# Indirect transfers of a routed expert layer without a bound: empty slots point at 256 spare rows

## The chip, the cores and the metric

The kernel runs on one core of one Trainium2 chip. The time is device time of one launch in microseconds (us). A core has five engines with instruction streams of their own: TensorE (PE, with its weight loads PEld), VectorE (DVE), ScalarE (ACT), GpSimd (POOL) and SyncE (SP), and 16 DMA engines that move what the queues give them. "POOLq", "SPq" or "DVEq" in a row is the stream of an engine where it does no work of its own kind: it sets a register or issues a transfer.

## The reference

Four blocks follow one another on 4096 tokens (16 x 256) of width 256: causal attention, a ternary feed-forward layer, attention with relative positions, and a layer with 64 routed experts. Only the last one is touched here. Its core, cut to what matters:

```python
scores = jax.nn.sigmoid(x @ gate_w.T)                 # 4096 x 64
topw, topi = jax.lax.top_k(scores, K)                 # K = 8 experts for each token
topw = topw / topw.sum(-1, keepdims=True)
# pos: running number of a token within its expert, C = 256 places for each expert
buf = jnp.zeros((E, C, h)).at[e_flat, pos].set(xin, mode='drop')
g = jax.nn.silu(jnp.einsum('ech,eih->eci', buf, expert_wg))
u = jnp.einsum('ech,eih->eci', buf, expert_wu)
out_buf = jnp.einsum('eci,ehi->ech', g * u, expert_wd)
rows = out_buf[e_flat, pos]
routed = (rows.reshape(T, K, h) * topw[..., None]).sum(1)
return (shared + routed).reshape(b, s, h)
```

There are 64 x 256 = 16384 slots. A token that comes after the 256th of its expert reads the last slot's result. With the inputs of this case the reference's routing puts a token into 11711 slots and leaves 4673 empty: 35 experts are full, 29 are not (one has no token at all).

## The kernel before

`expert_ffn` has two blocks, with a barrier of all engines between them.

The first block (names that begin with m_) works through the tokens in R = 8 rounds of 512. It normalises them, computes gate and shared expert, and writes two tables in device memory: `rows_w`, one row of 320 numbers for each token (256 of the normalised token, 64 gate weights), and `base`, the token plus the shared expert's result. It also makes the map from slots to tokens: `k_token`, 128 x 128 whole numbers, one for each slot. The map comes out of a matmul (`ps_map`), goes through device memory (`slot_map`) to be turned, and three DVE instructions then end the block: an empty slot stands as 0 in the turned map, a filled one as token + 1. `empty` is BIG = 2^20 where the map is below 0.5 and else 0, `map_T` is the sum of both, and `k_token` is `map_T` minus 1. So an empty slot points at row 2^20 - 1. POOL fills the seven buffers `k_rows` with zeros at the end of its part (L1781).

The second block (names that begin with e_) runs over the experts. For expert e the engines do this:

- POOL gathers the rows of its 256 slots with two indirect transfers of 128 rows (L2092, `gather(e)`) into one of seven buffers `k_rows`, 1280 bytes a row. It runs AHEAD = 6 experts ahead.
- PE turns the rows (L2173), multiplies with the expert's three weight matrices (L2184, L2196), which SP loads (L2071 to L2073); ACT and DVE make silu and product between (L2150, L2128).
- ACT copies the result to `e_y`, of which there are two buffers, scaled with the gate weight that stands in the gathered row (L2157). It first waits until the scatter of expert e - 2 has landed.
- POOL adds the result's 256 rows of 1024 bytes into a table of sums with two indirect transfers that accumulate (L2106). Even experts add into `base_scratch`, odd ones into `slots_in_scratch`, so that two experts in flight never add to the same row.

The order on POOL is written out by hand: 6 gathers of two transfers, then for each e the gather of e + 6 and the scatter of e. Each indirect transfer carries a bound:

```python
pool.indirect_dma_start(out=rows[u][:, c, :], out_offset=None, in_=rows_w,
                        in_offset=bass.IndirectOffsetOnAxis(ap=token[:, e * C + c:e * C + c + 1], axis=0),
                        bounds_check=T - 1, oob_is_err=False).then_inc(gathered[u], 16)
```

A row whose number is above the bound is skipped, without an error. The bound is a register, which POOL's stream sets ahead of each transfer (the rows POOLq MOVE of L2092 and L2106).

After the last scatter has landed, both tables are read back, added, completed by the rows of late tokens, and written out (L2080, L2081, L2135, L2140, L2161).

Of the kernel before, what the change touches and what calls it, by code (L numbers as in the profile page):

```python
# [6 lines left out]
F32 = mybir.dt.float32  # L7
# [3 lines left out]
ALU = mybir.AluOpType  # L11
# [3 lines left out]
P = 128  # L15
B, S, D = 16, 256, 256
# [3 lines left out]
T = B * S  # L20
EPS = 1e-5
START = 5
# [29 lines left out]
def bcast(ap, n):  # L52

    return ap.unsqueeze(1).to_broadcast([ap.shape[0], n, ap.shape[1]])
# [1581 lines left out]
def expert_ffn(nc, x3, g_ffn, gate_w, s_wg, s_wu, s_wd, e_wg, e_wu, e_wd, out, slots_in, slots_out, base, pick, weight):  # L1636
# [6 lines left out]
    E, TOP, CAP = gate_w.shape[1], 8, 256  # L1643
    I = s_wg.shape[1]
    G = 4
    R = T // (G * P)
    N = G * P
    C = CAP // P
    K16 = 16
    W = D + E  # L1650
    ROUND = 1.5 * 2.0 ** 23
    BIG = 2.0 ** 20
    rows_w = nc.dram_tensor("rows_w_scratch", (T, W), F32, kind="Internal").ap()
    slot_map = nc.dram_tensor("slot_map_scratch", (E * C, P), F32, kind="Internal").ap()
    sums = [base.rearrange("b s d -> (b s) d"), slots_in[0:T]]
    keep = ExitStack()
    ident = keep.enter_context(nc.sbuf_tensor("k_ident", [P, P], F32))
    late_T = keep.enter_context(nc.sbuf_tensor("k_late_T", [E, T], F32))
    token = keep.enter_context(nc.sbuf_tensor("k_token", [P, E * C], U32))
    ROWS = 7  # L1660
    rows = [keep.enter_context(nc.sbuf_tensor(f"k_rows{i}", [P, C, W], F32)) for i in range(ROWS)]
    with ExitStack() as stack:
# [4 lines left out]
        def sem(name):  # L1667
            sems.append(stack.enter_context(nc.semaphore("m_" + name)))
            return sems[-1]
# [3 lines left out]
        digit = sb("digit", [P, K16], F32)  # L1673
        QE = E // 4
        is_high, is_low = sb("is_high", [P, QE, K16, 4], BF16), sb("is_low", [P, QE, K16, 4], BF16)
        own_p = sb("own_p", [P, 1], F32)
        gate_t = sb("gate_t", [P, ND, E], F32)
        swg, swu, swd = sb("swg", [P, ND, I], F32), sb("swu", [P, ND, I], F32), sb("swd", [I, D], F32)
        gate, tanh_g = sb("gate", [P, 2], F32), sb("tanh_g", [P, 2], F32)
# [29 lines left out]
        weight_ready, late_ready, late_turned, late_copied = (sem("weight_ready"), sem("late_ready"), sem("late_turned"),  # L1709
                                                              sem("late_copied"))  # L1710
        high_ready, low_ready, mapped = sem("high_ready"), sem("low_ready"), sem("mapped")
        blanked = sem("blanked")
        own_ready, tile_ready = sem("own_ready"), sem("tile_ready")
        row_written, base_written = [sem(f"row_written{i}") for i in range(2)], sem("base_written")
        map_ready, map_written, map_loaded, map_turned, token_ready = (
            sem(n) for n in ("map_ready", "map_written", "map_loaded", "map_turned", "token_ready"))
        block = stack.enter_context(nc.Block())
        tiles = lambda a: a.rearrange("b (t p) d -> (b t) p d", p=P).rearrange("(r g) p d -> r p g d", g=G)
        x_rows, base_rows = tiles(x3), tiles(base)
        w_rows = rows_w.rearrange("(r g p) w -> r p g w", g=G, p=P)  # L1720
        wide = lambda a: a[:].rearrange("p g e -> p (g e)")

        @block.sync
        def _(sp):
            for s in sems:
                sp.sem_inc(s, START)
            sp.dma_start(x_in[0][:], x_rows[0]).then_inc(x_loaded, 16)
            sp.dma_start(gate_t[:], gate_w.rearrange("(t p) n -> p t n", p=P)).then_inc(const_loaded, 16)
            for dst, src in ((swg, s_wg), (swu, s_wu)):
                sp.dma_start(dst[:], src.rearrange("(t p) n -> p t n", p=P)).then_inc(const_loaded, 16)  # L1730
            sp.dma_start(swd[:], s_wd).then_inc(const_loaded, 16)
            sp.dma_start(gate[:], g_ffn.partition_broadcast(P)).then_inc(const_loaded, 16)
            for r in range(R):
                if r + 1 < R:
                    sp.wait_ge(base_ready, START + 2 * r)
                    sp.wait_ge(x_loaded, START + 16 * (r + 1))
                    sp.dma_start(x_in[(r + 1) % 2][:], x_rows[r + 1]).then_inc(x_loaded, 16)
                sp.wait_ge(xn_ready, START + r * G + G)
                sp.wait_ge(weight_ready, START + r + 1)
                sp.dma_start(w_rows[r], row[r % 2][:]).then_inc(row_written[r % 2], 16)  # L1740
                sp.wait_ge(base_ready, START + 2 * r + 2)
                sp.dma_start(base_rows[r], x_base[:]).then_inc(base_written, 16)
            sp.wait_ge(map_ready, START + 1)
            for j in range(4):
                sp.dma_start(slot_map.rearrange("(g j c) p -> j (c p) g", j=4, c=C).rearrange("j (a b) g -> j a g b", b=K16)[j],
                             map_p[32 * j:32 * j + K16, :, :]).then_inc(map_written, 16)
            sp.wait_ge(map_written, START + 64)
            sp.dma_start(map_in[:], slot_map).then_inc(map_loaded, 16)
            for i in range(2):
                sp.wait_ge(row_written[i], START + 16 * R // 2)  # L1750
            sp.wait_ge(base_written, START + 16 * R)
            sp.wait_ge(token_ready, START + 1)

        @block.gpsimd
        def _(pool):
            pool.memset(ident[:], 0.0).then_inc(pool_step, 1)
            pool.memset(before[:], 0.0).then_inc(pool_step, 1)
            pool.wait_ge(pool_step, START + 2)
            pool.affine_select(out=ident[:], in_=ident[:], compare_op=ALU.not_equal, fill=1.0, base=0,
                               pattern=[[-1, P]], channel_multiplier=1).then_inc(const_made, 1)  # L1760

            pool.affine_select(out=before[:], in_=before[:], compare_op=ALU.is_ge, fill=1.0, base=0,
                               pattern=[[-1, P]], channel_multiplier=1).then_inc(const_made, 1)
            pool.memset(neg_half[:], -0.5).then_inc(const_made, 1)
            pool.memset(ones[:], 1.0).then_inc(const_made, 1)
            pool.memset(nulls[:], 0.0).then_inc(const_made, 1)
            pool.iota(digit[:], [[1, K16]], base=0, channel_multiplier=0,
                      allow_small_or_imprecise_dtypes=True).then_inc(const_made, 1)
            pool.iota(own_p[:], [[1, 1]], base=1, channel_multiplier=1,
                      allow_small_or_imprecise_dtypes=True).then_inc(const_made, 1)  # L1770

            def invert(r):
                pool.wait_ge(var_ready, START + r + 1)
                pool.tensor_tensor(rstd[:], moments[:, :, 1], neg_half[:], ALU.pow).then_inc(rstd_ready, 1)

            invert(0)
            for r in range(R):
                if r + 1 < R:
                    invert(r + 1)
            for u in range(ROWS):  # L1780
                pool.memset(rows[u][:], 0.0).then_inc(blanked, 1)  # L1781
            pool.wait_ge(blanked, START + ROWS)

        @block.vector
        def _(dve):
# [119 lines left out]
            own.wait()  # L1905
            dve.scalar_tensor_tensor(map_p[:], map_t[:], float(P), ps_vals[:, :, 0, :], ALU.mult, ALU.add).then_inc(map_ready, 1)
            dve.wait_ge(map_turned, START + 1)
            own.step(dve.tensor_scalar(empty[:], ps_turn[0][:, 0:E * C], 0.5, BIG, ALU.is_lt, ALU.mult))
            own.wait()
            own.step(dve.tensor_tensor(map_T[:], ps_turn[0][:, 0:E * C], empty[:], ALU.add))  # L1910
            own.wait()
# [117 lines left out]
    with ExitStack() as stack:  # L2029
# [27 lines left out]
        sums_loaded, out_written = ([sem(f"{n}{i}") for i in range(NB)] for n in ("sums_loaded", "out_written"))  # L2057
        block = stack.enter_context(nc.Block())
        up = lambda a: a.rearrange("e (t p) i -> e p t i", p=P) if len(a.shape) == 3 else a.rearrange("(e t p) i -> e p t i", e=E, p=P)
        sum_rows = [a.rearrange("(r p g) d -> r p g d", g=G, p=P) for a in sums]  # L2060
        out_rows = out.rearrange("b s d -> (b s) d").rearrange("(r p g) d -> r p g d", g=G, p=P)
        late_banks = (ps_turn, ps_gu)

# [19 lines left out]
        @block.gpsimd  # L2083
        def _(pool):
            def gather(e):
                u = e % ROWS
                if e >= ROWS:
                    pool.wait_ge(turned, START + e - ROWS + 1)
                    pool.wait_ge(y_copied, START + C * (e - ROWS + 1))
                pool.sem_inc(tick, 1)  # L2090
                for c in range(C):
                    pool.indirect_dma_start(out=rows[u][:, c, :], out_offset=None, in_=rows_w,  # L2092
                                            in_offset=bass.IndirectOffsetOnAxis(ap=token[:, e * C + c:e * C + c + 1], axis=0),
                                            bounds_check=T - 1, oob_is_err=False).then_inc(gathered[u], 16)

            for e in range(AHEAD):
                gather(e)
            for e in range(E):
                if e + AHEAD < E:
                    gather(e + AHEAD)  # L2100
                pool.wait_ge(y_copied, START + C * (e + 1))
                if e >= 2:
                    pool.wait_ge(scattered[e % 2], 32 * (e // 2))
                pool.sem_inc(tick, 1)
                for c in range(C):
                    pool.indirect_dma_start(out=sums[e % 2],  # L2106
                                            out_offset=bass.IndirectOffsetOnAxis(ap=token[:, e * C + c:e * C + c + 1], axis=0),
                                            in_=y[e % 2][:, c * D:(c + 1) * D], in_offset=None, bounds_check=T - 1,
                                            oob_is_err=False, compute_op=ALU.add).then_inc(scattered[e % 2], 16)
            for i in range(2):  # L2110
                pool.wait_ge(scattered[i], 32 * E // 2)

# [152 lines left out]
```

## Time and profile before

| | |
|---|---|
| median of 3 runs | 2313.06 us (2312.68 to 2321.97) |
| the profiled execution's own time | 2309.97 us |
| its span in the profile | 2308.1 us |
| second block of `expert_ffn` | 1848.5 to 2308.1 us |
| loop over the experts, from the first scatter on | 1868.2 to 2267.4 us |
| POOL busy in the span | 656.3 us (28%) |

A row of instruction groups shows the line of the kernel, the engine, the operation, what it writes and reads, and its time. The busy share of POOL over the whole span says little, since three quarters of its work stand in the last fifth of the span; the table of stretches shows that.

### The profile page before, as it was taken

Reading aid. Unit: us, or ns where it says so; the run is one execution under the profiler, and the core shown is the slowest. Engines: PE = TensorE matmul, PEld = TensorE weight load, DVE = VectorE, ACT = ScalarE, POOL = GpSimd, SP = SyncE. Lnnn points to the kernel's source line nnn. Section 1 sums busy time; section 2 is a strip of 40 time slices with the busy share of each in tenths; the row PEclk is TensorE's granted clock in tenths of the full one; section 3 lists DMA queues with packets and bytes.
Section 4 is the critical chain, followed back from the end, with each engine's and each line's share of the span. In section 5 each row is a group of like instructions: output and inputs, shape, how many; then the busy total and the mean of one; then the engine's idle time right before and its main releaser. Section 6 shows DMA issues by size and latency. Waiting matters only on the chain. (4 is left out here: it accounts for less than half of the span.)

```text
span 2308.1 us, 52796 instructions
## 1 busy us (share of the span) xinstructions
PE 1738.1 (75%) x22308; PEld 1329.5 (58%) x22308; DVE 1258.5 (55%) x2416; ACT 793.1 (34%) x1420; POOL 656.3 (28%) x594
## 2 busy tenths in 40 slices
PE   5999999379564889888889887795566576677665
PEld 3777776268543667666667665674344354455443
DVE  5766666267332768666776677684477521111113
ACT  2555554133131443344334433342165411111110
POOL 2121211067420110021011101101000078888882
PEclk9999999689875788778878877787677589988896
DMA  6787875213245123322322232101122156565567
GB/s 139 151 153 139 145 139 96 78 64 101 62 133 110 47 75 57 66 66 74 66 60 70 67 76 42 43 21 29 61 71 81 45 143 129 116 135 121 124 123 237
DMA packets 224844, 216.79 MB, mean 94 GB/s; under 512 B 62724, under 2 KB 200430, under 8 KB 224096
## 3 DMA queue, kind: packets, MB, share of 16 engines
q1 hardware_dynamic: 194080, 179.01, 32.9%
q0 software_dynamic: 24576, 27.05, 6.9%
q10 hardware_dynamic: 5952, 7.35, 0.9%
q8 instruction: 177, 2.90, 0.5%
q14 instruction: 59, 0.48, 0.1%
HBM read 147.08 MB, written 72.45 MB: 95 GB/s over the span
## 5 line engine op out<-in xcount | busy, mean ns | idle before, releaser
L2128 DVE TENSOR_TENSOR e_hT<-e_sil,e_ps_gu 128x256 f32<-128x256 f32 x64 | 26.9, 421 | 323.4 <-ACT e_sil L2150 323.4
L1316 DVE TENSOR_TENSOR r_score<-r_ps_s,r_score 128x512 f32<-128x512 f32 x256 | 172.2, 689 | 47.1 <-PE r_ps_s L1566 42.9
L2157 ACT ACTIVATE e_y<-e_ps_y,k_rows 128x256 f32<-128x256 f32 x128 | 53.7, 471 | 323.3 <-DMA base_scratch<-e_y,k_token 162.4
L1535 PE MATMUL r_ps_s<-r_q,r_rk 96*128 96x64 bf16 x2048 | 148.6, 236 | 20.3 <-DMA r_q<-parts_scratch 13.0
L1176 POOL TENSOR_TENSOR r_avT<-r_avT,r_w 128x1024 f32<-128x1024 f32 x16 | 37.7, 2355 | 439.4 <-DMA r_w<-r_w_raw 439.4
L2092 POOL DMA_INDIRECT k_rows<-rows_w_scratch,k_token x128 | 135.0, 1055 | 90.7 <-issue 90.4
L1286 DVE TENSOR_TENSOR r_score<-r_score,r_ps_t 128x1024 f32<-128x1024 f32 x128 | 154.2, 1215 | 10.6 <-PE r_ps_t L1546 9.9
L332 DVE TENSOR_REDUCE a_row_max<-a_ps_max 128x2 f32<-128x512 f32 (+1 forms) x192 | 130.3, 685 | 53.1 <-PE a_ps_max L482 28.7
L1535 PEld LDWEIGHTS r_ps_s<-r_q,r_rk 96*128 96x128 bf16 x2048 | 128.0, 120 | 48.1 <-issue 20.3
L1406 ACT ACTIVATE r_score<-r_ps_s 128x512 f32<-128x512 f32 x192 | 111.5, 601 | 113.0 <-PE r_ps_s L1535 111.8
L1566 PE MATMUL r_ps_s<-r_q,r_k 96*128 96x64 bf16 x2048 | 115.0, 203 | 46.3 <-DMA r_k<-parts_scratch 32.1
L1393 ACT ACTIVATE r_score<-r_score 128x1024 f32<-128x1024 f32 x128 | 136.1, 1063 | 29.9 <-DVE r_score L1286 28.6
L424 ACT ACTIVATE a_p<-a_ps_exp 128x512 f32<-128x512 f32 x192 | 111.7, 595 | 86.8 <-PE a_ps_exp L503 61.5
L2193 PE MATMUL e_ps_last<-e_wd,e_h_last 128*64 128x256 f32 x128 | 43.2, 422 | 120.6 <-DVE e_h_last L2129 119.0
L1566 PEld LDWEIGHTS r_ps_s<-r_q,r_k 96*128 96x128 bf16 x2048 | 84.7, 103 | 78.4 <-DMA r_k<-parts_scratch 33.0
L1588 PE MATMUL r_ps_b<-r_score,r_v_all 128*32 128x64 f32 x4096 | 118.2, 238 | 0.0
L1613 PE MATMUL r_ps_b<-r_score,r_rv 128*32 128x64 f32 x4096 | 104.5, 244 | 12.0 <-issue 12.0
L2106 POOL DMA_INDIRECT base_scratch<-e_y,k_token x64 | 102.4, 1600 | 20.7 <-issue 19.0
L1333 DVE TENSOR_REDUCE r_row_max<-r_ps_t 128x4 f32<-128x512 f32 x128 | 88.3, 690 | 36.1 <-PE r_ps_t L1602 35.4
L2106 POOL DMA_INDIRECT slots_in_scratch<-e_y,k_token x64 | 102.4, 1600 | 19.5 <-issue 19.2
L1613 PEld LDWEIGHTS r_ps_b<-r_score,r_rv 128*32 128x32 f32 x4096 | 78.3, 115 | 39.5 <-issue 39.5
L694 POOL TENSOR_TENSOR f_h_lo<-f_h,f_h_hi 128x512 fp32r<-128x512 f32 x64 | 88.7, 1391 | 34.2 <-DVE f_h_hi L765 34.2
(299 smaller groups left out, 4163.4 us busy)
## 6 DMA issues: line engine op xcount, KB each, us to landing
a_q<-parts_scratch SPq DMA_DIRECT2D x96, 128.0 KB, 4.2
a_k<-parts_scratch SPq DMA_DIRECT2D x96, 128.0 KB, 7.0
r_q<-parts_scratch SPq DMA_DIRECT2D x96, 128.0 KB, 3.1
e_wg<-in_L_ffn_expert_wg SPq DMA_DIRECT2D x64, 128.0 KB, 2.4
e_wu<-in_L_ffn_expert_wu SPq DMA_DIRECT2D x64, 128.0 KB, 3.1
e_wd<-in_L_ffn_expert_wd SPq DMA_DIRECT2D x64, 128.0 KB, 3.4
r_k<-parts_scratch SPq DMA_DIRECT2D x4, 1536.0 KB, 14.3
rows_w_scratch<-m_row SPq DMA_DIRECT2D x8, 640.0 KB, 3.2
```

The costliest lines, as they stand in the source:

```text
L332: dve.tensor_reduce(row_max[:, t, h0:h0 + n], ps_max[s % 2][:].rearrange("p (h k) -> p h k", h=n), AX.X, ALU.max).then_inc(maxed, 1)
L424: act.activation(out.rearrange("p h q -> p (h q)"), ps_exp[c % 2][:], ACT.Exp).then_inc(expd, 1)
L1286: dve.tensor_tensor(part, part, bcast(ps_t[m % 2][:], NT), ALU.add).then_inc(shifted, 1)
L1316: dve.tensor_tensor(part, ps_s[c % 2][:].rearrange("p (c e q) -> p c q e", c=4, e=2), part, ALU.add).then_inc(added, 1)
L1393: act.activation(part, part, ACT.Exp, scale=float(DH) ** -0.5).then_inc(expd, 1)
L1406: act.activation(by_query[1 - par][:, c // 8, :, q0:q0 + 8, :], ps_s[c % 2][:].rearrange("p (q c e) -> p c q e", c=HC, e=2), ACT.Copy).the ...
L1535: ins = pe.matmul(ps_s[c % 2][:, n * BH:(n + 1) * BH], rk6[:, j:j + P], q_now[:, :, q, :], start=True, stop=True)
L1566: ins = pe.matmul(ps_s[c % 2][:, n * CQ:(n + 1) * CQ], k6[:, h0 + n, k * P:(k + 1) * P], q_now[:, (h0 + n) // 2, :, n % 2], start=True, st ...
L1588: ins = pe.matmul(ps_b[g // 8][32 * j:32 * j + 32, (g % 8) * CQ:(g % 8 + 1) * CQ], v_all[:, first:first + 32], by_query[par][:, k, hd // 2 ...
L1613: ins = pe.matmul(out, rv[:, m * DH:m * DH + 32], by_query[par][:, k, :, q, :], start=(k == 0), stop=(k == NT - 1), skip_group_check=True, ...
L2092: pool.indirect_dma_start(out=rows[u][:, c, :], out_offset=None, in_=rows_w, in_offset=bass.IndirectOffsetOnAxis(ap=token[:, e * C + c:e * ...
L2106: pool.indirect_dma_start(out=sums[e % 2], out_offset=bass.IndirectOffsetOnAxis(ap=token[:, e * C + c:e * C + c + 1], axis=0), in_=y[e % 2 ...
```

## The change

The bound goes, and no slot points outside a table any more. `rows_w` grows by 256 rows (CAP = 256), which are filled with zeros from the blank buffer `k_rows` 0. An empty slot number 128c + p of any expert now points at row 4096 + 128c + p: `null_row`, made once on POOL, holds that number plus 1 for p down and c across, and takes the place of BIG. Both tables of sums get 256 more rows, which no one reads; since `base` has none to spare, the even experts' table moves to the first 4352 rows of `slots_out_scratch`, a scratch tensor that was not used before.

```diff
-    BIG = 2.0 ** 20
-    rows_w = nc.dram_tensor("rows_w_scratch", (T, W), F32, kind="Internal").ap()
+    rows_w = nc.dram_tensor("rows_w_scratch", (T + CAP, W), F32, kind="Internal").ap()
-    sums = [base.rearrange("b s d -> (b s) d"), slots_in[0:T]]
+    base = slots_out[0:T]
+    sums = [slots_out[0:T + CAP], slots_in[0:T + CAP]]
...
@@ first block, SP, after the rounds
+            sp.wait_ge(blanked, START + ROWS)
+            sp.dma_start(rows_w[T:T + CAP, :].rearrange("(c p) w -> p c w", c=C), rows[0][:]).then_inc(null_written, 16)
             sp.wait_ge(map_ready, START + 1)
...
+            sp.wait_ge(null_written, START + 16)
             sp.wait_ge(base_written, START + 16 * R)
...
@@ first block, POOL, among its constants
+            pool.iota(null_row[:], [[P, C]], base=T + 1, channel_multiplier=1,
+                      allow_small_or_imprecise_dtypes=True).then_inc(null_made, 1)
...
@@ first block, DVE, at its end
             dve.wait_ge(map_turned, START + 1)
-            own.step(dve.tensor_scalar(empty[:], ps_turn[0][:, 0:E * C], 0.5, BIG, ALU.is_lt, ALU.mult))
+            dve.wait_ge(null_made, START + 1)
+            own.step(dve.scalar_tensor_tensor(empty[:].rearrange("p (e c) -> p e c", c=C), ps_turn[0][:, 0:E * C].rearrange("p (e c) -> p e c", c=C),
+                                              0.5, bcast(null_row[:], E), ALU.is_lt, ALU.mult))
...
@@ second block, POOL
                     pool.indirect_dma_start(out=rows[u][:, c, :], out_offset=None, in_=rows_w,
-                                            in_offset=bass.IndirectOffsetOnAxis(ap=token[:, e * C + c:e * C + c + 1], axis=0),
-                                            bounds_check=T - 1, oob_is_err=False).then_inc(gathered[u], 16)
+                                            in_offset=bass.IndirectOffsetOnAxis(ap=token[:, e * C + c:e * C + c + 1], axis=0)).then_inc(gathered[u], 16)
...
-                                            in_=y[e % 2][:, c * D:(c + 1) * D], in_offset=None, bounds_check=T - 1,
-                                            oob_is_err=False, compute_op=ALU.add).then_inc(scattered[e % 2], 16)
+                                            in_=y[e % 2][:, c * D:(c + 1) * D], in_offset=None, compute_op=ALU.add).then_inc(scattered[e % 2], 16)
```

The order of the instructions stays as it was, but for two that are put in. On SP, at the end of the first block, the program reads as follows (- is before, + is the changed one; `m_row` goes to the table of tokens, `m_x_base` to the even experts' table):

```order
 L1740 DMA rows_w_scratch<-m_row 128x4x320
-L1742 DMA base_scratch<-m_x_base 128x4x256
-L1745 DMA slot_map_scratch<-m_map_p 16x16x16 x4
-L1748 DMA m_map_in<-slot_map_scratch 128x128
+L1742 DMA slots_out_scratch<-m_x_base 128x4x256
+L1744 DMA rows_w_scratch<-k_rows 128x2x320
+L1747 DMA slot_map_scratch<-m_map_p 16x16x16 x4
+L1750 DMA m_map_in<-slot_map_scratch 128x128
```

The transfer of the zero rows stands after the last round's two stores and ahead of the map's way through device memory; nothing else changed its place.

On DVE, at the end of the first block, the map becomes `k_token`. Before:

```order
L1904 COPY m_map_t<-m_ps_map 128x256
L1906 SCALAR_TENSOR_TENSOR m_map_p<-m_map_t,m_ps_map 128x256
L1908 TENSOR_SCALAR m_empty<-m_ps_turn 128x128
L1910 TENSOR_TENSOR m_map_T<-m_ps_turn,m_empty 128x128
L1912 TENSOR_SCALAR k_token<-m_map_T 128x128
```

and after the change:

```order
L1909 COPY m_map_t<-m_ps_map 128x256
L1911 SCALAR_TENSOR_TENSOR m_map_p<-m_map_t,m_ps_map 128x256
L1914 SCALAR_TENSOR_TENSOR m_empty<-m_ps_turn,m_null_row 128x128
L1917 TENSOR_TENSOR m_map_T<-m_ps_turn,m_empty 128x128
L1919 TENSOR_SCALAR k_token<-m_map_T 128x128
```

One instruction has another form and reads a second operand; none is added. On POOL one instruction is added among the constants of the first block (`m_null_row`), and the loop's transfers keep their order.

## Rows read from the trace of the kernel before

**Rows 1.** The page's first part, busy time and share of the span by engine.

```profile
span 2308.1 us, 52796 instructions
PE 1738.1 (75%) x22308; PEld 1329.5 (58%) x22308; DVE 1258.5 (55%) x2416; ACT 793.1 (34%) x1420; POOL 656.3 (28%) x594
```

**Rows 2.** Busy time by stretch: before, start, loop, loop without gathers, end.

```profile
core 0: us, PE busy (x) PEld busy (x) DVE busy (x) ACT busy (x) POOL busy (x), PEclk, DMA share, GB/s
0.00:1848.50 1848.50, 1431.45 (x21092) 1109.12 (x21092) 1167.92 (x2199) 721.32 (x1228) 316.56 (x338) 0.82 0.37 82
1848.50:1868.20 19.70, 11.65 (x46) 9.21 (x46) 3.67 (x8) 1.61 (x4) 14.29 (x15) 0.64 0.52 147
1868.20:2245.20 377.00, 260.96 (x1076) 186.78 (x1075) 64.39 (x177) 65.20 (x175) 306.81 (x230) 0.91 0.60 128
2245.20:2267.40 22.20, 12.42 (x50) 8.95 (x48) 2.48 (x8) 5.02 (x13) 18.66 (x12) 0.96 0.49 53
2267.40:2308.10 40.70, 21.63 (x48) 15.48 (x48) 20.08 (x24) 0.00 (x0) 0.00 (x0) 0.50 0.87 313
```

**Rows 3.** POOL in order of time, two experts (start us, duration us, idle before).

```profile
1999.12 1.63 POOL L2106 DMA_INDIRECT base_scratch<-e_y,k_token  x1 [0.30 <-issue]
2001.06 1.58 POOL L2106 DMA_INDIRECT base_scratch<-e_y,k_token  x1 [0.30 <-issue]
2002.94 1.07 POOL L2092 DMA_INDIRECT k_rows<-rows_w_scratch,k_token  x1 [0.30 <-issue]
2004.32 1.04 POOL L2092 DMA_INDIRECT k_rows<-rows_w_scratch,k_token  x1 [0.31 <-issue]
2005.67 1.63 POOL L2106 DMA_INDIRECT slots_in_scratch<-e_y,k_token  x1 [0.30 <-issue]
...
2012.22 1.63 POOL L2106 DMA_INDIRECT base_scratch<-e_y,k_token  x1 [0.30 <-issue]
```

**Rows 4.** ACT in order of time, the same stretch.

```profile
2005.49 0.84 ACT L2157 ACTIVATE e_y<-e_ps_y,k_rows 128x256 f32<-128x256 f32 x2 [5.60 <-DMA base_scratch<-e_y,k_token]
2011.93 0.84 ACT L2157 ACTIVATE e_y<-e_ps_y,k_rows 128x256 f32<-128x256 f32 x2 [5.33 <-DMA slots_in_scratch<-e_y,k_token]
```

**Rows 5.** The scatter's line L2106: durations in ns (min/median/max), who waited, landing.

```profile
L2106 POOL DMA_INDIRECT base_scratch<-e_y,k_token x64: 1552/1582/1629, 1868.2 to 2262.1; - x64
L2106 POOL DMA_INDIRECT slots_in_scratch<-e_y,k_token x64: 1553/1582/1646, 1874.7 to 2265.8; - x64
  ACT e_y L2157: 320.8, 62
DMA to landing us min/median/max: 2.7/3.9/4.8
```

**Rows 6.** The gather's line L2092, the same view.

```profile
L2092 POOLq MOVE  x128: 29/29/38, 1847.6 to 2231.4; - x128
L2092 POOL DMA_INDIRECT k_rows<-rows_w_scratch,k_token x128: 994/1044/1284, 1848.5 to 2240.1; - x128
```

**Rows 7.** L2106 between 2004.2 and 2012.5 us, the register moves among them.

```profile
L2106 POOL DMA_INDIRECT slots_in_scratch<-e_y,k_token x2: 1581/1604/1627, 2005.7 to 2007.6; - x2
L2106 POOLq MOVE  x2: 29/29/29, 2006.5 to 2007.0; - x2
```

**Rows 8.** DMA queues from 1850 us on: packets, MB, share of 16 engines.

```profile
q0 software_dynamic: 24576, 27.05, 35.0%
```

**Rows 9.** The start: POOL's first scatter, and ACT's first copies of a result.

```profile
1868.17 1.62 POOL L2106 DMA_INDIRECT base_scratch<-e_y,k_token  x1 [1.44 <-ACT e_y L2157]
1866.43 0.84 ACT L2157 ACTIVATE e_y<-e_ps_y,k_rows 128x256 f32<-128x256 f32 x2 [1.25 <-PE e_ps_y L2196]
1870.23 0.84 ACT L2157 ACTIVATE e_y<-e_ps_y,k_rows 128x256 f32<-128x256 f32 x2 [1.25 <-PE e_ps_y L2196]
1857.66 1.11 PE L2173 MATMUL e_ps_turn<-k_ident,k_rows 128*128 128x128 f32 x4 [2.93 <-DMA k_rows<-rows_w_scratch,k_token]
```

**Rows 10.** Busy time of two stretches of 26.2 us: few filled slots, and many.

```profile
1999.10:2025.30 26.20, 17.01 (x72) 12.25 (x72) 4.45 (x13) 5.25 (x15) 21.30 (x16) 0.93 0.50 120
2064.70:2090.90 26.20, 15.59 (x73) 11.11 (x72) 4.35 (x12) 4.88 (x14) 21.32 (x17) 1.00 0.66 135
```

**Rows 11.** The end of the first block: DVE and SP in order of time.

```profile
1846.20 0.29 DVE L1908 TENSOR_SCALAR m_empty<-m_ps_turn 128x128 f32<-128x128 f32 x1 [5.54 <-PE m_ps_turn L2026]
1846.53 0.29 DVE L1910 TENSOR_TENSOR m_map_T<-m_ps_turn,m_empty 128x128 f32<-128x128 f32 x1
1827.81 0.36 SPq L1742 DMA_DIRECT2D base_scratch<-m_x_base  x1
1840.69 1.87 SPq L1745 DMA_DIRECT2D slot_map_scratch<-m_map_p  x4
```

**Rows 12.** The last experts: POOL's last scatter and its predecessor, ACT's last copies.

```profile
2241.41 1.63 POOL L2106 DMA_INDIRECT slots_in_scratch<-e_y,k_token  x1 [0.30 <-issue]
2260.19 1.55 POOL L2106 DMA_INDIRECT base_scratch<-e_y,k_token  x1 [0.35 <-issue]
2265.77 1.55 POOL L2106 DMA_INDIRECT slots_in_scratch<-e_y,k_token  x1 [0.31 <-issue]
2258.49 0.84 ACT L2157 ACTIVATE e_y<-e_ps_y,k_rows 128x256 f32<-128x256 f32 x2 [2.68 <-DMA base_scratch<-e_y,k_token]
```

More of the change, by code:

```diff
@@ L1675, in expert_ffn @@
         is_high, is_low = sb("is_high", [P, QE, K16, 4], BF16), sb("is_low", [P, QE, K16, 4], BF16)
-        own_p = sb("own_p", [P, 1], F32)
+        own_p, null_row = sb("own_p", [P, 1], F32), sb("null_row", [P, C], F32)
         gate_t = sb("gate_t", [P, ND, E], F32)
@@ L1711, in expert_ffn @@
         high_ready, low_ready, mapped = sem("high_ready"), sem("low_ready"), sem("mapped")
-        blanked = sem("blanked")
+        blanked, null_made, null_written = sem("blanked"), sem("null_made"), sem("null_written")
         own_ready, tile_ready = sem("own_ready"), sem("tile_ready")
@@ L1718, in expert_ffn @@
         tiles = lambda a: a.rearrange("b (t p) d -> (b t) p d", p=P).rearrange("(r g) p d -> r p g d", g=G)
-        x_rows, base_rows = tiles(x3), tiles(base)
-        w_rows = rows_w.rearrange("(r g p) w -> r p g w", g=G, p=P)
+        x_rows, base_rows = tiles(x3), base.rearrange("(r g p) d -> r p g d", g=G, p=P)
+        w_rows = rows_w[0:T].rearrange("(r g p) w -> r p g w", g=G, p=P)
         wide = lambda a: a[:].rearrange("p g e -> p (g e)")
@@ L2059, in expert_ffn @@
         up = lambda a: a.rearrange("e (t p) i -> e p t i", p=P) if len(a.shape) == 3 else a.rearrange("(e t p) i -> e p t i", e=E, p=P)
-        sum_rows = [a.rearrange("(r p g) d -> r p g d", g=G, p=P) for a in sums]
+        sum_rows = [a[0:T].rearrange("(r p g) d -> r p g d", g=G, p=P) for a in sums]
         out_rows = out.rearrange("b s d -> (b s) d").rearrange("(r p g) d -> r p g d", g=G, p=P)
```

## The prediction

> **What bounds the kernel now.** I read the page's busy shares first. There POOL is the least busy engine, 28% of the span [rows 1]. The table of stretches corrects that: in the loop over the experts (1868.2 to 2245.2 us) POOL is busy 306.8 of 377 us, 81%, while PE has 69%, DVE and ACT 17% each, and the DMA engines 60% [rows 2]. POOL in order of time then shows where the other 19% are: ahead of every transfer stand 0.30 us of "issue", in which POOL waits for no one [rows 3]. One expert is two gathers (1.07 and 1.04 us), two scatters (1.63 and 1.58) and four gaps of 0.30: 6.52 us, and the trace has 2012.22 - 2005.67 = 6.55 us from one expert's scatter to the next [rows 3]. So nothing but POOL's own instructions sets this loop's pace. From the first scatter at 1868.17 to that of expert 57 at 2241.41 [rows 9, 12] are 57 intervals of 6.548 us.
>
> The view of line L2106 says that ACT waited 320.8 us for landed scatters [rows 5], which looks like a bound. It is not one: ACT's copies start at 2005.49 and 2011.93 and take 0.84 us [rows 4]. The scatter at 2005.67 belongs to expert 21, so the copy of 2005.49 is expert 22's, which POOL takes up at 2012.22: it lies ready for 2012.22 - 2006.33 = 5.9 us. The rest of the pipeline could go faster as well: before the scatters hold it back, ACT's copies are 1870.23 - 1866.43 = 3.80 us apart [rows 9].
>
> What the change can win is therefore POOL's time for an indirect transfer, 256 times. What it can lose is in the transfers themselves, once they eat up 5.9 us of reserve.
>
> **How many transfers count.** I call s what one transfer gets shorter on POOL. At the start 14 gathers stand ahead of the first scatter, but POOL already waits 1.44 us there for ACT [rows 9], of which 0.30 is the usual gap; that copy hangs on the gathers of experts 0 and 1 (PE turns expert 1's rows only at 1857.66, after a wait for the gather). So only some 3 of the 14 pay. Behind the first scatter stand 57 intervals of two gathers and two scatters, and then 14 scatters to the end: 3 + 114 = 117 gathers and 114 + 14 = 128 scatters, 245 in all. In the part without gathers an expert takes 2 x (1.55 + 0.31) = 3.7 us, and ACT's copy ends at 2259.33, 0.86 us ahead of its scatter at 2260.19, 0.5 us when the gap is taken off [rows 12]. There s above about 0.25 would not be paid in full; that touches 14 transfers and I neglect it.
>
> **What a bound costs.** No row shows an indirect transfer without one, so I bound s from both sides.
> - The register move: 29 ns [rows 6], 256 of them, 7.4 us if they lay on the path. They don't: the two moves of L2106 at 2006.5 and 2007.0 us fall within the transfer that runs from 2005.67 to 2007.30 [rows 7, 3]. I count 0.
> - The gap of 0.30 us: it is the same after gathers and after scatters, and I leave it.
> - The comparison of 128 numbers with the bound. POOL's time does not depend on how many rows are skipped: in a stretch with many empty slots POOL is busy 21.30 us and in one with full experts 21.32 us, 16 transfers each, while the DMA share goes from 0.50 to 0.66 [rows 10]. So a skipped row costs POOL what a real one does, and filling the empty slots costs POOL nothing. It also means that the check is done in straight line over all rows, whatever it finds. Lower end: it is free, s = 0. I see no reason for less than nothing, since the instruction asks for strictly less. Upper end: a scatter takes 1.58 us and a gather 1.04 us for the same 128 rows [rows 5, 6]; the 0.54 us are a whole additional step for each row (the old sum is read too), 4.2 ns a row. Comparing and selecting is a small part of such a step. I take a sixth, s = 0.09 us, 0.7 ns a row; this is a choice between 0 and 0.54, nearer to the bottom because a step that reads a further row does more than compare. For the range I take 0.22, two fifths.
>
> 245 x 0.09 = 22 us less. The ends are 0 and 245 x 0.22 = 54 us; with the whole 0.54 it would be 132.
>
> A rule speaks against any gain. Where the Trainium skill (DMA: Bandwidth & Descriptors, section "Anatomy of one DMA — SWDGE (gpsimd) path") splits a transfer's fixed time, it calls descriptor generation "small, variable", with many descriptors to be had before a cost shows. By that rule a cheaper generation wins nothing and the time stays at 2313. The trace does not bear out that it is small here, with 1.04 and 1.58 us a transfer and 81% of the loop; it leaves open that the check alone is.
>
> **What is added.**
> - Real traffic for empty slots. The queue of indirect transfers moves 27.05 MB [rows 8]. At 1280 + 1024 bytes for a slot that is read and added these are 11.7 thousand slots, so 4.6 thousand more come, 10.7 MB, 40% more on this queue. Its share of the DMA engines is 35.0% of 458 us, 160 us; 40% of that are 63 us, 16 points in a loop of 399 us: 0.60 becomes about 0.76. Stretches of full experts run at 0.66 today, at the same pace [rows 10]. Price 0. The cover is the 5.9 us of reserve. The cycle that must hold over two experts is: second scatter 1.93 us after the first, L until it lands, copy 0.84, gap 0.30, so 3.07 + L below 13.1 us, or L below 10 us. L is 3.9 us at the median and 4.8 at most [rows 5].
> - The zero rows' transfer on SP (L1744). SP issued its last store at 1827.81 and then had nothing to do until 1840.69 [rows 11]; an issue takes 0.36 us there. The new transfer falls into these 12.5 us, and the blank buffers are ready before. Nothing waits behind it. Price 0, or 0.4 us if it were late.
> - DVE's `empty` becomes an instruction with a second operand. `map_T`, which also reads two operands of 128x128, takes 0.29 us, as the old form does [rows 11]. It stands on the path to the first gather. Price 0 to 0.1 us. The wait for `null_made`, an iota in the first block's beginning, is long over; queued behind it are only the three instructions to `k_token`, for which POOL waits.
> - The even experts' table lies in another tensor, with the same shape of rows. Price 0.
>
> **Sum.** 2309.97 - 22 + 0 = 2288 us for the profiled execution. The median of the runs shown lies 3.1 us above that execution, so I forecast 2291 us, 0.95% below 2313.06. The interval from scatter to scatter would go from 6.55 to about 6.19 us.
>
> **Rivals.** Differences below 0.5% (11.6 us) are about what a measurement of this kernel cannot tell from none.
> - The check costs next to nothing. For it: the flat time of POOL at any number of skipped rows [rows 10] fits wide instructions in which a comparison drowns. Against it: nothing but the size of 1 us for 128 rows. For all s below 0.047 us (245 x 0.047 = 11.6): 2302 to 2313. Chance 0.32.
> - The check costs much, s above 0.22: below 2259. The gather would have to lose over a fifth of its time. Chance 0.08.
> - Slower: the scatters to spare rows land late. All 29 experts that are not full now add to the same 256 rows of two tables, where the skipped rows moved nothing. If such additions took L from 3.9 to above 10 us, ACT's copy, and with it POOL's next scatter, would come late by (L - 10)/2 for each of those experts: L = 11 gives 2313 + 29 x 0.5 = 2328 with no gain from s. It decides from L = 10 on. Against it: within a transfer every empty slot has a row of its own, the two transfers of an expert use different rows, and an expert's scatter goes out only after that of e - 2 into the same table has landed; full experts have L of 3.9 today. Chance 0.07, and 0.01 for something unseen that is as slow.
>
> **How the numbers follow.** s between 0.047 and 0.22 has 0.52 (2259 to 2301), above that 0.08, below 0.32, slower 0.08. Faster by over 0.5%: 0.60, within 0.32, slower 0.08. The range runs from 2259 (s = 0.22) to 2316 (no gain, 0.5 us of additions and what runs differ by), and leaves out 0.08 at each end.
>
> **What the profile of the changed kernel would show.** Right: gathers' median near 0.95 us instead of 1.044, scatters' near 1.49 instead of 1.582, gaps of 0.30 as before, no register moves; 37.7 MB on the indirect queue; DMA share near 0.76 in the loop; landing of scatters below 5 us; ACT's copies still some 5 us ahead of their scatters; the first block unchanged to 0.5 us. Wrong would be: durations as before (the check is free), a smaller gap in place of shorter transfers (the cost sat in the issue), or POOL waiting for ACT ahead of scatters (the slower rival). The prediction falls with the size of s, which no row fixes.

## The result and the profile after

| | before | changed |
|---|---|---|
| median of 19 runs | 2316.76 us | 2309.46 us |
| lowest to highest | 2309.28 to 2327.39 | 2293.57 to 2317.25 |
| span of the profiled execution | 2308.1 us | 2312.2 us |
| from the first indirect transfer's start to the last one's | 417.26 us | 410.20 us |
| one expert's scatter to the next, mean of 57 | 6.548 us | 6.432 us |

The ratio is 0.9966, with a 95% interval of 0.995 to 0.9982: faster by 0.34%, where 0.95% was forecast. In the medians that is 7.3 us, and by the interval 4 to 12 us. The time lies within the range, but only because the range reached up to no gain at all; the gain is a third of what I worked out.

The profiled execution of the changed kernel is 4.1 us longer than that of the one before. The table of stretches says where: the code ahead of the second block, in which only a handful of instructions differ, ended at 1858.2 instead of 1848.5 us; the indirect transfers took 7.1 us less; and what follows the last of them took 1.4 us more. Its columns are those of [rows 2].

```profile
core 0: us, PE busy (x) PEld busy (x) DVE busy (x) ACT busy (x) POOL busy (x), PEclk, DMA share, GB/s
0.00:1858.20 1858.20, 1437.30 (x21092) 1113.98 (x21092) 1167.92 (x2199) 720.50 (x1228) 316.52 (x339) 0.82 0.36 82
1858.20:1877.40 19.20, 11.53 (x45) 9.13 (x46) 3.67 (x8) 1.61 (x4) 13.53 (x14) 0.64 0.69 205
1877.40:2247.80 370.40, 263.18 (x1077) 188.18 (x1076) 64.48 (x177) 65.05 (x175) 300.35 (x230) 0.90 0.73 155
2247.80:2270.10 22.30, 12.33 (x49) 8.89 (x47) 2.48 (x8) 5.01 (x13) 18.66 (x12) 0.96 0.62 71
2270.10:2312.20 42.10, 22.02 (x48) 15.38 (x48) 20.08 (x24) 0.00 (x0) 0.00 (x0) 0.50 0.84 303
```

That first stretch is where executions of one kernel differ: in the profiled executions of this study it ends anywhere between 1847.3 and 1858.3 us. Here the delay was there before the first added transfer: SP's last store ahead of it (L1742) went out at 1837.35 instead of 1827.81 us.

```profile
1837.35 0.36 SPq L1742 DMA_DIRECT2D slots_out_scratch<-m_x_base  x1
1837.76 0.50 SPq L1744 DMA_DIRECT2D rows_w_scratch<-k_rows  x1
1850.23 2.14 SPq L1747 DMA_DIRECT2D slot_map_scratch<-m_map_p  x4
```

The stretch from the first to the last indirect transfer is far steadier (417.3, 417.9 and 417.5 us for three kernels with bounded gathers; 410.2, 410.2, 411.0 and 410.0 us for four executions with unbounded ones), so I read the changes there, and the whole times only over many runs.

The changed kernel's views of the gather's line (L2099) and the scatter's (L2112), with durations in ns, answer to [rows 5, 6]:

```profile
L2099 POOL DMA_INDIRECT k_rows<-rows_w_scratch,k_token x128: 942/982/1222, 1858.3 to 2242.7; - x128
```

```profile
L2112 POOL DMA_INDIRECT slots_out_scratch<-e_y,k_token x64: 1553/1586/1628, 1877.4 to 2264.7; - x64
L2112 POOL DMA_INDIRECT slots_in_scratch<-e_y,k_token x64: 1552/1587/1643, 1883.8 to 2268.5; - x64
  ACT e_y L2162: 312.4, 61
DMA to landing us min/median/max: 3.7/3.9/5.4
```

The three numbers are the shortest, the median and the longest. The reader is to see one thing: a gather went from 1044 to 982 ns at the median, a scatter from 1582 to 1586. Only half of the transfers became shorter, and those by 0.06 us. POOL in order of time shows the same, and the gap of 0.30 us as it was:

```profile
1997.02 1.02 POOL L2099 DMA_INDIRECT k_rows<-rows_w_scratch,k_token  x1 [0.30 <-issue]
1998.34 0.98 POOL L2099 DMA_INDIRECT k_rows<-rows_w_scratch,k_token  x1 [0.30 <-issue]
1999.63 1.62 POOL L2112 DMA_INDIRECT slots_in_scratch<-e_y,k_token  x1 [0.30 <-issue]
2001.56 1.59 POOL L2112 DMA_INDIRECT slots_in_scratch<-e_y,k_token  x1 [0.30 <-issue]
...
2006.06 1.62 POOL L2112 DMA_INDIRECT slots_out_scratch<-e_y,k_token  x1 [0.30 <-issue]
```

The sum by the measured terms: 57 intervals are 57 x 0.116 = 6.6 us shorter, the start (first gather to first scatter) 19.17 instead of 19.66 us, 0.5 us shorter: 7.1 us. The medians differ by 7.3 us; with an interval of 4 to 12 us around it, the closeness of the two is in part luck.

The indirect queue moves 37.77 MB, 16384 gathered rows and 16384 scattered ones, and its share of the DMA engines from 1850 us on rose from 35.0% [rows 8] to 46.0%:

```profile
q0 software_dynamic: 24576, 37.77, 46.0%
```

ACT's copies still lie ready well ahead: that of 2011.89 is done at 2012.73, and POOL takes it up at 2018.93.

### The profile page after: what moved, and what is told of

Read it like the earlier page. It is cut to its first block and busy times, and to the rows that moved or that the text cites. A ratio compares the mean times of both kernels' runs of the same rounds, so it can differ in the third digit from the quotient of the medians.

```text
span 2312.2 us, 52545 instructions
## 1 busy us (share of the span) xinstructions
PE 1746.4 (76%) x22308; PEld 1335.6 (58%) x22308; DVE 1258.6 (54%) x2416; ACT 792.2 (34%) x1420; POOL 649.1 (28%) x595
## 3 DMA queue, kind: packets, MB, share of 16 engines
q0 software_dynamic: 24576, 37.77, 9.2%
## 5 line engine op out<-in xcount | busy, mean ns | idle before, releaser
L2099 POOL DMA_INDIRECT k_rows<-rows_w_scratch,k_token x128 | 127.6, 997 | 90.8 <-issue 90.2
L2112 POOL DMA_INDIRECT slots_out_scratch<-e_y,k_token x64 | 102.4, 1601 | 20.9 <-issue 18.9
L2112 POOL DMA_INDIRECT slots_in_scratch<-e_y,k_token x64 | 102.5, 1601 | 19.6 <-issue 19.6
```

The costliest lines, as they stand in the source:

```text
L2112: pool.indirect_dma_start(out=sums[e % 2], out_offset=bass.IndirectOffsetOnAxis(ap=token[:, e * C + c:e * C + c + 1], axis=0), in_=y[e % 2 ...
```

## The experiments

Two quantities are compared: the ratio to the kernel before over several rounds, and the time from the first to the last indirect transfer in the profile ("the transfers' stretch" below; 417.3 us before, 410.2 changed). e1, e2, e3 and the changed kernel are the four combinations of bounded and unbounded gathers and scatters. e4, e5 and e6 ran once each and serve for the durations alone: they overwrite, leave out rows or add where the kernel should not, so their sums are others.

**e1: the spare rows stay, the bound comes back.**

```diff
-    in_offset=bass.IndirectOffsetOnAxis(ap=token[:, e * C + c:e * C + c + 1], axis=0)).then_inc(gathered[u], 16)
+    in_offset=bass.IndirectOffsetOnAxis(ap=token[:, e * C + c:e * C + c + 1], axis=0),
+    bounds_check=T + CAP - 1, oob_is_err=False).then_inc(gathered[u], 16)
```

and the same on the scatters.

> The changed kernel with its spare rows, but every indirect transfer carries a bound of 4351 again (skip mode), which no slot exceeds. Theory A (the bound itself costs POOL 0.06 us in a gather and nothing in a scatter): gathers back at 1.044 us median, scatters at 1.58, 6.55 us from one expert's scatter to the next, time equal to the kernel before within 1 us or so (2316). Theory B (the gathers are shorter because no row is skipped any more, not because the bound is gone): gathers stay at 0.98, interval 6.43, time as the changed kernel (2309). If the added traffic of the spare rows costs anything, this kernel is slower than the one before by that much.

Measured: 1.0004 (0.9988 to 1.0019), the transfers' stretch 417.9 us.

```profile
L2099 POOL DMA_INDIRECT k_rows<-rows_w_scratch,k_token x128: 997/1048/1285, 1852.7 to 2244.8; - x128
```

The gather is back at 1048 ns although no row is skipped. So the bound is what costs, not the skipping; theory B falls. And the 10.7 MB of added traffic, which this kernel has too, cost nothing that can be measured: the interval of the ratio leaves room for some 3 us down and 4 us up.

**e2: a bound on the scatters alone (4095), so that empty slots are not added.**

> Gathers without a bound, from the table with spare rows; scatters with the bound 4095 as before, so that empty slots are skipped in the adds. Theory A: gathers 0.98 us, scatters 1.58, interval 6.43, time as the changed kernel within 1 us: 0.3% below the kernel before; the 4673 additions that fall away save nothing, since POOL sets the pace. Rival C (the additions to spare rows cost something at the edges, in the last landing or the start): 1 to 3 us below the changed kernel.

Measured: 0.9969 (0.9951 to 0.9987), the stretch 411.0 us, gathers 985 ns, scatters 1587 ns. This is the whole gain of the change, within the intervals. Rival C finds no support: without the additions to spare rows the stretch is 0.8 us longer, not shorter. Run again as e10:

> e2 once more, on the same chip as e9: 411 us from the first to the last indirect transfer, 0.3% below the kernel before, and 6 to 7 us above e9.

It gave 0.9975 (0.9957 to 0.9992) and 410.0 us.

**e3: a bound on the gathers alone (4095).**

> Gathers with the bound 4095 as before (skipped rows keep what an earlier expert left in the buffer; its result goes to spare rows that no one reads), scatters without a bound. Theory A: gathers 1.044, scatters 1.58, interval 6.55, time as the kernel before. Were a scatter's bound worth as much as a gather's, the interval would be 6.43 and the time 7 us less.

Measured: 1.0000 (0.998 to 1.0019), the stretch 417.5 us, gathers 1048 ns, scatters 1581 ns.

```profile
L2111 POOL DMA_INDIRECT slots_out_scratch<-e_y,k_token x64: 1552/1581/1630, 1870.7 to 2265.0; - x64
L2111 POOL DMA_INDIRECT slots_in_scratch<-e_y,k_token x64: 1554/1581/1647, 1877.2 to 2268.8; - x64
```

Half of the edit is worth nothing that shows: the scatter's bound is free. Its median is 1581 with a bound (e1) and without (e3) where gathers are bounded, and 1586 or 1587 either way where they are not (e2, e10, the changed kernel), so the 4 ns between 1582 and 1586 go with the gathers, not with the scatter's own bound.

**e4: which form costs what.** Gathers by e % 4 and scatters by e // 4 % 4, each form on a line of its own (given in short, not as code; "plain" overwrites instead of adding):

```diff
+    if e % 4 == 0: gather without a bound                                       # L2100
+    elif e % 4 == 1: bounds_check=T + CAP - 1, oob_is_err=False                 # L2102
+    elif e % 4 == 2: bounds_check=T + CAP - 1                                   # L2104
+    elif e % 4 == 3: bounds_check=T - 1, oob_is_err=False                       # L2106
...
+    if e // 4 % 4 == 0: compute_op=ALU.add                                      # L2119
+    elif e // 4 % 4 == 1: compute_op=ALU.add, bounds_check=T + CAP - 1, oob_is_err=False  # L2121
+    elif e // 4 % 4 == 2: plain                                                 # L2123
+    elif e // 4 % 4 == 3: plain, bounds_check=T + CAP - 1, oob_is_err=False     # L2125
```

> Forms mixed by expert, each on a line of its own: gathers without a bound, with the bound 4351 in skip mode, with 4351 in error mode, with 4095 in skip mode; scatters that add without and with a bound (4351, skip), and plain scatters that overwrite instead of adding, without and with the bound (half of the experts overwrite, so the sums are not the reference's). Theory A: gathers 0.98 without, 1.04 in all three bounded forms, whatever the limit and the mode. On scatters, A1 (adding hides the check: the list of reads, twice as long, is what takes the time, and the check is done beside it): plain scatters are near 1.0 us and differ by 0.06 between with and without a bound, adding ones by nothing. A2 (in a scatter the check is hidden by the direction, not by the addition): plain scatters differ by nothing either. If the mode matters (theory D: the gather's 0.06 us pay for skipping, not for comparing), the error-mode gathers take 0.98.

Measured, the line views of the gathers and of one table's scatters:

```profile
L2100 POOL DMA_INDIRECT k_rows<-rows_w_scratch,k_token x32: 951/982/1202, 1857.1 to 2197.4; - x32
L2102 POOL DMA_INDIRECT k_rows<-rows_w_scratch,k_token x32: 998/1034/1072, 1859.8 to 2203.8; - x32
L2104 POOL DMA_INDIRECT k_rows<-rows_w_scratch,k_token x32: 1017/1057/1099, 1862.5 to 2210.4; - x32
L2106 POOL DMA_INDIRECT k_rows<-rows_w_scratch,k_token x32: 1002/1038/1076, 1865.1 to 2215.7; - x32
L2119 POOL DMA_INDIRECT slots_in_scratch<-e_y,k_token x16: 1579/1602/1627, 1883.0 to 2181.0; - x16
L2121 POOL DMA_INDIRECT slots_in_scratch<-e_y,k_token x16: 1579/1604/1627, 1909.1 to 2207.1; - x16
L2123 POOL DMA_INDIRECT slots_in_scratch<-e_y,k_token x16: 956/984/1019, 1934.0 to 2224.6; - x16
L2125 POOL DMA_INDIRECT slots_in_scratch<-e_y,k_token x16: 983/1002/1017, 1955.0 to 2235.6; - x16
```

A bounded gather costs 52 to 56 ns more in skip mode, whatever the limit, and 75 ns more in error mode, in which a number above the bound counts as an error instead of being skipped; so theory D falls. A plain scatter takes 0.98 us, as a gather does, and its bound costs 18 ns (15 on the other table): a third of the gather's, neither the 0.06 of A1 nor the nothing of A2. With the addition it costs 2 ns or less. I had not expected this middle value.

**e5: is it paid by row or by transfer?** Transfers of 64 rows beside those of 128 (gathers L2100 to L2106, the last two of 64 rows; adding scatters L2119 to L2125 likewise; the second of each two has the bound). The edit in short:

```diff
+  rows[u][0:64, c, :] <- token[0:64, ...]      (e % 4 in 2, 3)
+  y[e % 2][0:64, ...] -> token[0:64, ...]      (e // 4 % 4 in 2, 3)
```

> The changed kernel with four kinds of gather by expert: 128 rows without and with a bound (4351, skip), and the first 64 rows alone without and with it; the same four kinds of adding scatters. Half of the experts leave out half of their rows, so the result is not the reference's. Theory A (the bound costs per row): a gather of 64 rows takes near 0.6 us and the bound adds 0.03 us to it, against 0.055 at 128. Rival (the bound costs once for each transfer: the register is read, another path is taken): it adds the same 0.055 us at 64 rows. Adding scatters: 64 rows near 0.9 us, bound and none alike.

```profile
L2100 POOL DMA_INDIRECT k_rows<-rows_w_scratch,k_token x32: 962/993/1221, 1853.6 to 2211.3; - x32
L2102 POOL DMA_INDIRECT k_rows<-rows_w_scratch,k_token x32: 999/1045/1071, 1856.4 to 2217.8; - x32
L2104 POOL DMA_INDIRECT k_rows<-rows_w_scratch,k_token x32: 916/950/962, 1859.0 to 2224.2; - x32
L2106 POOL DMA_INDIRECT k_rows<-rows_w_scratch,k_token x32: 952/994/1000, 1861.5 to 2230.3; - x32
L2119 POOL DMA_INDIRECT slots_in_scratch<-e_y,k_token x16: 1578/1590/1633, 1880.0 to 2195.5; - x16
L2123 POOL DMA_INDIRECT slots_in_scratch<-e_y,k_token x16: 1412/1438/1476, 1931.1 to 2240.2; - x16
```

Half the rows shorten a gather by 43 ns of 993, 0.7 ns a row, and an adding scatter by 152 ns of 1590, 2.4 ns a row. The rest, 0.91 and 1.29 us by a straight line through the two sizes, is paid for each transfer. The bound costs 52 ns at 128 rows and 44 ns at 64, where theory A has half and the rival all of it. So the rival is nearer: by the same line 36 of the 52 ns are paid once for each transfer and 16 by row; with only two sizes this is an estimate. My expectation of 0.6 and 0.9 us for half a transfer was far off (0.95 and 1.44).

**e6: does the addition hide the check, or the direction?** Gathers by e % 4: plain, plain with a bound, adding (L2104), adding with a bound (L2106).

> The changed kernel with four kinds of gather by expert: plain without and with a bound (4351, skip), and gathers that add to what stands in the buffer, without and with it; the adding ones make the result another than the reference's. Theory A1 (the addition hides the check): an adding gather takes near 1.55 us, and with a bound no more. Theory A2 (what counts is which side the row numbers are on: they point at the source in a gather and at the target in a scatter): the adding gather grows with a bound by about as much as the plain one, 0.05 us.

```profile
L2104 POOL DMA_INDIRECT k_rows<-rows_w_scratch,k_token x32: 1537/1554/1602, 1862.5 to 2268.3; - x32
L2106 POOL DMA_INDIRECT k_rows<-rows_w_scratch,k_token x32: 1537/1562/1577, 1866.2 to 2275.9; - x32
```

The adding gather takes 1554 ns and with a bound 1562, beside 995 and 1040 for the plain ones. So with an addition the bound's price all but goes, in either direction, as A1 has it. The direction counts too, though: without an addition the bound costs a gather 45 to 56 ns (e4, e6) and a scatter 15 to 18 (e4).

**e7 to e9: a change of kind.** "Kind" is gather or scatter. e2 with POOL's order by pairs of experts:

```diff
-                if e + AHEAD < E:
-                    gather(e + AHEAD)
+                if e % 2 == 0:
+                    for n in (e + AHEAD, e + AHEAD + 1):
+                        if n < E:
+                            gather(n)
```

> Gathers without a bound, scatters with 4095 (as e2), and POOL's order by pairs of experts: four gathers, then four scatters. The traces show a gather at 0.95 us in the row of gathers at the start and at 1.02 and 0.98 between scatters, a scatter at 1.55 after scatters and at 1.63 and 1.59 after gathers. Theory S (the change of kind costs: the first two transfers after it are 0.07 and 0.04 us longer): the third and fourth of a run take 0.95 and 1.55 to 1.57, an expert's mean interval goes from 6.43 to about 6.33 us, 6 us less in all, near 2301. Rival (the durations are longer in the loop because of the load of weights or of the other engines): they stay as they are, and so does the time.

Measured: 0.9948 (0.9928 to 0.9968), the stretch 403.5 us. POOL in order of time:

```profile
1998.22 1.02 POOL L2099 DMA_INDIRECT k_rows<-rows_w_scratch,k_token  x1 [0.31 <-issue]
1999.55 0.98 POOL L2099 DMA_INDIRECT k_rows<-rows_w_scratch,k_token  x1 [0.30 <-issue]
2000.83 0.95 POOL L2099 DMA_INDIRECT k_rows<-rows_w_scratch,k_token  x1 [0.30 <-issue]
2002.09 0.95 POOL L2099 DMA_INDIRECT k_rows<-rows_w_scratch,k_token  x1 [0.30 <-issue]
2003.34 1.63 POOL L2114 DMA_INDIRECT slots_out_scratch<-e_y,k_token  x1 [0.30 <-issue]
2005.27 1.59 POOL L2114 DMA_INDIRECT slots_out_scratch<-e_y,k_token  x1 [0.30 <-issue]
2007.16 1.56 POOL L2114 DMA_INDIRECT slots_in_scratch<-e_y,k_token  x1 [0.30 <-issue]
2009.02 1.57 POOL L2114 DMA_INDIRECT slots_in_scratch<-e_y,k_token  x1 [0.30 <-issue]
```

The third and fourth of a run are short, amid the same load of the other engines: theory S holds for the durations. The time, 2305.35 us, is above the 2301 expected. Beside it the changed kernel ran once more on the same chip:

> The changed kernel once more, on the same chip as e7, so that e7 is compared with it directly: gathers 0.98, scatters 1.58, time 0.3% below the kernel before.

It gave 0.9973 (0.9952 to 0.9995) and 410.2 us. The medians, 2305.35 for e7 and 2307.76 for e8, are only 2.4 us apart and the intervals of their ratios overlap; the stretch, 6.7 us apart, is the sharper reading.

e9 lets the pairs begin with expert 1:

> As e7 (gathers without a bound, scatters with 4095, POOL's order by pairs), but expert 0 is scattered alone after 14 gathers, and the pairs begin with expert 1. In e7 two more gathers stand ahead of the first scatter, which comes 1.8 us later after the first gather than in the changed kernel (21.0 against 19.2 us). Theory S: from the first to the last indirect transfer 403.5 us in e7 against 410.2 in the changed kernel; here the start's 1.8 us come back only as far as they were idle time, since the same transfers are issued in all: 402.5 to 403.5, time within 1 us of e7 and 0.5 to 0.6% below the kernel before. If the total is below 402, something else than the number of changes of kind counts.

Measured: 0.9942 (0.9921 to 0.9962), median 2302.91 beside 2309.47 for e10 on the same chip, the stretch 404.1 us, a little more than I expected and no better than e7's 403.5: POOL waited 1.65 us for ACT ahead of its first scatter there, which e7 fills with gathers. The order by pairs is faster than the kernel before in both runs. Beside kernels with unbounded gathers its stretch is 6.7 us (e7 and the changed kernel) and 5.9 us (e9 and e10) shorter, and in e9 the median is 6.6 us lower; in e7 the medians alone would not show it. Which start is better can't be told apart.

## Why the prediction was wrong in size

- **What bounds the loop: right.** POOL's transfers and gaps add up to the interval before and after, and each kernel's stretch follows its transfers' durations.
- **How many transfers count: right for the loop, open for the start.** 114 gathers in the 57 intervals gave 6.6 us, 0.058 each. The start was to give 3 gathers' worth, 0.2 us, and gave 0.5; but it lasts 18.96 to 19.65 us in the four executions with unbounded gathers and this order, and 19.40 to 19.68 in the three with bounded ones, so its share isn't fixed. 117 x 0.062 = 7.3 us, beside 7.1 in the stretch, is as close as this can be told.
- **What a bound costs: the step that failed**, in two ways. It gave one s to all 245 transfers; the 128 scatters have s = 0 (e3, and the adding forms in e4 and e6). And it chose 0.09 us for the gathers, which have 0.06. 245 x 0.09 = 22 us should have been 117 x 0.062 + 128 x 0 = 7.3 us. Of the 18 us between 2291 and the measured 2309.46, the kernel before accounts for 3.7: its median was 2313.06 in the three runs shown and is 2316.76 over 19.
- **Why the choice was wrong.** It rested on the reading that the 0.54 us between a scatter and a gather are work by row, 4.2 ns each, and the check a sixth of it. e4 shows that the 0.54 us belong to the addition, not to the scatter: a plain scatter takes 0.98 us like a gather. e5 shows that rows are cheap: 0.7 ns each in a gather, 2.4 ns in an adding scatter, with 0.91 and 1.29 us for each transfer. The larger part of the bound's cost comes by transfer too. It was the one term that no row gave, and I had no ground to give the adding transfers the same one; a case of "gathers gain, scatters don't" stood in none of the rivals.
- **The first rival came true in number.** 7.3 us over 245 transfers are 0.030 us each, below its 0.047, and 2309.46 lies in its 2302 to 2313. Its reason, that a comparison drowns in wide instructions, is not what the runs show: in the gathers the bound costs 0.06 us, clear of noise. And 0.34% could be told from none over 19 runs, where the prediction took 0.5% for the limit.
- **The register move and the gap: right.** Both counted 0; the moves are gone in the changed kernel and the gap is 0.30 us still.
- **Filling the empty slots: right.** POOL's time hardly changed with it (gathers 1044 and 1048 ns, scatters 1582 and 1581 before and in e1), the DMA share of the loop rose from 0.60 to 0.73 where I wrote 0.76, and L stayed at 3.9 us, 5.4 at most, below the 10 us from which it would decide. The slower rival fell with that. (The two stretches of [rows 10] hold 16 and 17 transfers, not 16 each: the ends of the second cut two. The reading stands.)
- **The additions ahead of the loop: right.** The zero rows went out at 1837.76 us for 0.50 us, while the map was ready for SP only at 1850.23; the three DVE instructions take 0.29, 0.29 and 0.23 us. From SP's last store (L1742) to the first gather are 20.9 us, where 20.7 were before, and 20.5 in e10, which has the same additions.
- **The rule of the Trainium skill** (DMA: Bandwidth & Descriptors, "Anatomy of one DMA — SWDGE (gpsimd) path") that descriptor generation is small and that many descriptors fit in before a cost shows: for the cost of another row e5 agrees, 64 more gathered rows cost 0.04 us. For an adding scatter they cost 0.15 us. By transfer POOL's time is not small, 0.91 and 1.29 us, and the bound's part of it was won; there the measurement differs from the rule, and the measurement decides.

What stays open is why an addition hides the bound. The expectation of e4 has a picture for it: two lists are made side by side, and in an adding transfer the list of reads is so long that a check beside it doesn't show. e6 speaks against it as it stands: the row numbers of a gather belong to the reads, so the check should lengthen just that list in an adding gather, and it adds 8 ns. The Trainium skill (Perfetto Trace Analysis, "DMA Instruction — SWDGE (GPSIMD)") says that two processors generate the descriptors and that the profiler's end is that of the last; no run here shows the two apart, and so no such picture is shown. Nor did I try whether the cost is the reading of the register or the check itself.

## What to carry to other kernels

Where indirect transfers set the pace, count them and their kinds before anything else: most of POOL's time is paid by transfer (0.91 of 0.99 us in a gather, 1.29 of 1.59 in an adding scatter) and the smaller part by row, so a saving has to be priced for each form by itself. Filling empty slots with real rows cost POOL nothing here, with the DMA engines 73% busy in the loop; how full they may be before it costs was not tried. Taking the bound off pays some 0.05 us on plain gathers, 0.02 us on plain scatters and nothing that shows on adding transfers. Putting transfers of one kind next to each other paid as much again in the stretch.

## What the runs showed of the hardware

- A gather of 128 rows of 1280 bytes takes POOL 0.98 us, of 64 rows 0.95; an adding transfer of either direction 1.55 to 1.61 us, a plain scatter of rows of 1024 bytes 0.98 or 0.99 (medians).
- A bound costs a gather 0.044 to 0.066 us in skip mode (medians of e1 to e6) and 0.075 in error mode (e4), a plain scatter 0.015 to 0.018 (e4); an adding transfer with a bound differs from one without by -0.012 to 0.008 us (e4 to e6).
- A skipped row costs POOL as much as a real one: gathers take 1044 ns with 4673 rows skipped and 1048 with none (e1).
- After a change between gather and scatter the first two transfers are longer: 1.02 and 0.98 instead of 0.95, 1.63 and 1.59 instead of 1.55 us (e7). What is behind it stays open.
